# Attention scores from two float32r parts of queries and keys, in two row halves of the array

## The reference

```python
x = x + _L0_attn_ref(_layernorm(x, axis=-1), ...)     # retention
x = x + _L0_ffn_ref(_layernorm(x, axis=-1), ...)      # experts
x = x + _L1_attn_ref(_layernorm(x, axis=-1), ...)     # attention
x = x + _L1_ffn_ref(_layernorm(x, axis=-1), ...)      # routed tokens
# _L1_attn_ref: 16 heads of 8 numbers
q = (hidden_states @ Wq.T + bq).reshape(b, s, 16, 8) * 8 ** -0.5
k = (hidden_states @ Wk.T + bk).reshape(b, s, 16, 8)
v = (hidden_states @ Wv.T + bv).reshape(b, s, 16, 8)
scores = jnp.einsum('bqhd,bkhd->bhqk', q, k)
probs = jax.nn.softmax(scores, axis=-1)
out = jnp.einsum('bhqk,bkhd->bqhd', probs, v).reshape(b, s, d) @ Wo.T + bo
```

## Time and profile before

| | us |
|---|---|
| median of 3 runs (1101.86 to 1104.05) | 1103.3 |
| span of the profiled execution | 1072.1 |
| what lies around the span (the difference) | 31.2 |
| first fill of the stacks to last (L1164) | 469.9 to 927.2 |

### The profile page before, as it was taken

The page is one execution under the profiler, slowest core; times in us unless marked ns, Lnnn a source line. Parts: engine busy times, 40 slices in busy tenths (PEclk is TensorE's granted clock), DMA queues, the critical chain, the costliest instruction groups (busy, mean ns, idle before and its releaser), DMA issues. The chain is left out here.

```text
span 1072.1 us, 29674 instructions
## 1 busy us (share of the span) xinstructions
PE 963.4 (90%) x9857; PEld 717.1 (67%) x9858; DVE 706.6 (66%) x1509; ACT 640.7 (60%) x1320; POOL 707.7 (66%) x1531
## 2 busy tenths in 40 slices
PE   6999999689989999459999999999999999963776
PEld 5888888479956666335767777777777777632554
DVE  5778787685534444236788887788787788735752
ACT  4666766422224434126788888888888888762552
POOL 4677676467735555567688888888888888534003
PEclk9999999799999999757999999999999999996999
DMA  8600000131123332134444544445454445302000
GB/s 315 262 3 2 2 2 2 45 104 53 50 74 83 81 83 70 52 106 132 122 137 140 149 130 141 127 137 150 124 149 124 124 134 140 99 17 61 12 3 21
DMA packets 88837, 100.91 MB, mean 94 GB/s; under 512 B 10654, under 2 KB 74366, under 8 KB 88318
## 3 DMA queue, kind: packets, MB, share of 16 engines
q1 hardware_dynamic: 83454, 87.97, 27.9%
q0 software_dynamic: 5248, 11.15, 3.2%
HBM read 61.78 MB, written 36.47 MB: 92 GB/s over the span
## 5 line engine op out<-in xcount | busy, mean ns | idle before, releaser
L1344 DVE TENSOR_REDUCE a_neg_max<-a_slot 128x4 f32<-128x1024 f32 x256 | 306.5, 1218 | 107.8 <-PE a_slot L1487 83.3
L1432 ACT ACTIVATE a_pT<-a_slot 128x1024 f32<-128x1024 f32 x256 | 255.3, 1024 | 13.5 <-PE a_slot L1503 6.5
L1487 PE MATMUL a_slot<-a_k_stack,a_q_stack 72*128 72x256 bf16 x1024 | 157.9, 278 | 7.3 <-DMA a_k_stack<-part_dram 6.3
L1503 PE MATMUL a_slot<-a_q_stack,a_k_stack 75*128 75x256 bf16 x1024 | 151.0, 275 | 2.0 <-ACT a_pT L1432 0.7
L1518 PE MATMUL a_ps_o<-a_pT,a_v_pad 128*32 128x256 f32 x2048 | 141.6, 386 | 0.0
L1487 PEld LDWEIGHTS a_slot<-a_k_stack,a_q_stack 72*128 72x128 bf16 x1024 | 95.5, 99 | 51.9 <-issue 25.5
L704 POOL DMA_INDIRECT y_rows<-m_total,m_token x80 | 76.6, 957 | 66.3 <-ACT m_total L857 52.4
L1503 PEld LDWEIGHTS a_slot<-a_q_stack,a_k_stack 75*128 75x128 bf16 x1024 | 93.0, 98 | 35.5 <-ACT a_pT L1432 14.2
L326 DVE TENSOR_TENSOR r_score<-ps_score,r_decay 128x512 f32<-128x512 f32 x128 | 81.4, 678 | 7.7 <-PE ps_score L478 7.6
L1518 PEld LDWEIGHTS a_ps_o<-a_pT,a_v_pad 128*32 128x32 f32 x2048 | 64.7, 109 | 27.5 <-issue 13.0
L697 POOL DMA_INDIRECT sorted_in<-h,m_slot x64 | 63.9, 998 | 26.1 <-issue 18.9
(11 more groups left out here) (293 smaller groups left out, 2121.7 us busy)
## 6 DMA issues: line engine op xcount, KB each, us to landing
a_q_stack<-part_dram SPq DMA_DIRECT2D x64, 288.0 KB
a_k_stack<-part_dram SPq DMA_DIRECT2D x64, 288.0 KB
part_dram<-a_part SPq DMA_DIRECT2D x64, 192.0 KB, 2.7
sorted_in<-h SPq DMA_DIRECT2D x10, 528.0 KB, 13.6
m_xe<-sorted_in SPq DMA_DIRECT2D x40, 132.0 KB, 2.2
expert_up<-in_eu_dram SPq DMA_DIRECT2D x1, 4096.0 KB, 25.1
part_dram<-a_part SPq DMA_DIRECT2D x64, 64.0 KB, 3.6
out_dram<-e_x_plus_h SPq DMA_DIRECT2D x32, 128.0 KB, 2.5
```

Of the source, the lines that this page charges most:

```text
L1344: nc.vector.tensor_reduce(neg_max[:, p, half, t, g * UNIT:(g + 1) * UNIT], slots[SLOT_OF["m", j]][:], AX.X, ALU.max, negate=True).then_inc ...
L1432: nc.scalar.activation(pT[:, j % PT_RING], slots[SLOT_OF["e", j]][:], ACT.Exp).then_inc(e_read, 1)
L1487: ins = nc.tensor.matmul(slots[SLOT_OF["m", j]][:, q], q_stack[0:QK_ROWS, p, half, head, t * P:(t + 1) * P], k_stack[0:QK_ROWS, p, half, h ...
L1503: ins = nc.tensor.matmul(slots[SLOT_OF["e", j]][:, q], k_stack[0:EXP_ROWS, p, half, head, t * P:(t + 1) * P], q_stack[0:EXP_ROWS, p, half, ...
```

## The change

- [...] The four products of parts take 4 x 8 = 32 rows; one row of zeros against ones follows (`MAX_ROWS` = 33), and two rows of maximum parts against ones (`EXP_ROWS` = 35).
- The 8 heads of a half are dealt to two row halves of the array (`TILES` = 2): rows 0 to 34 and rows 64 to 98 of the stacks. `scores` (L1490 of the new file) issues, for each group, the four matmuls alternately for the upper and the lower half; the two of a pair write different banks of the slot. The number of matmuls and their 128 x 256 output stay.
- The stacks and the DRAM buffers hold float32, 4 bytes for 2. A half's fill is four DMAs of 128 KB (two for `q_stack`, two for `k_stack`) instead of two of 288 KB. Keys and queries have a DRAM tensor each (`k_dram`, `q_dram`); a half's store is two DMAs of 64 KB for keys and one of 128 KB for queries, instead of one of 64 KB and one of 192 KB. A half's maxima take two DMAs instead of one.
- `k_stack` is filled from `k_dram` with the broadcast as the outermost dimension: the source is 2 (step 0) x 16 x 1024, the destination 32 rows x 1024. The source of `q_stack` is 16 x 2 (step 0) x 1024. Before, the sources were 24 x 3 x 2048 for both.
- `fill_ones` moves ahead of the first fill; the heads' order in the weights (`by_half`) follows the new layout; `ident_b` goes, since the maxima are transposed in float32.

```diff
 HH = AH // HALVES
-PARTS = 3
+PARTS = 2
 PAIRS = PARTS * PARTS
 QK_ROWS = PAIRS * AD
-EXP_ROWS = QK_ROWS + PARTS
+MAX_ROWS = QK_ROWS + 1
+EXP_ROWS = MAX_ROWS + PARTS
+TILES = 2
+TILE_ROWS = P // TILES
+HT = HH // TILES
 UNIT = 4
+UT = UNIT // TILES
 M_UNITS = AH // UNIT * TPS
 PT_RING = 4
...
         qk = m.sbuf("a_qk", [P, 2, 2, S])
-        rest = m.sbuf("a_rest", [P, 2, S])
-        part = m.sbuf("a_part", [P, 2, 2, PARTS, S], BF16)
-        SLOTS = 2 * PARTS + PARTS - 1
-        part_dram = nc.dram_tensor("part_dram", (2, HALVES, SLOTS, AD, HH, S), BF16, kind="Internal").ap()
-        q_stack = m.sbuf("a_q_stack", [P, 2, HALVES, HH, S], BF16)
-        k_stack = m.sbuf("a_k_stack", [P, 2, HALVES, HH, S], BF16)
+        part = m.sbuf("a_part", [P, 2, 2, PARTS, S])
+        q_dram = nc.dram_tensor("q_dram", (2, HALVES, PARTS, AD, HH, S), F32, kind="Internal").ap()
+        k_dram = nc.dram_tensor("k_dram", (2, HALVES, AD, PARTS, HH, S), F32, kind="Internal").ap()
+        q_stack = m.sbuf("a_q_stack", [P, 2, HALVES, HT, S])
+        k_stack = m.sbuf("a_k_stack", [P, 2, HALVES, HT, S])
...
-        max_rest = m.sbuf("a_max_rest", [P, TPS, HH])
-        max_part = m.sbuf("a_max_part", [P, HALVES, TPS, PARTS, HH], BF16)
-        max_T = m.sbuf("a_max_T", [PARTS * HH, HALVES, S], BF16)
+        neg_max = m.sbuf("a_neg_max", [P, 2, HALVES, TPS, TILES, HH // UNIT, UT])
+        max_part = m.sbuf("a_max_part", [P, HALVES, TPS, TILES, PARTS, HT])
+        max_T = m.sbuf("a_max_T", [PARTS * HH, HALVES, S])
         pT = m.sbuf("a_pT", [P, PT_RING, UNIT, S])
...
 
-        FILLS = 2
+        FILLS = 2 * TILES
+        STORES = 1 + PARTS
...
-                        for half in range(HALVES):
-                            sp.dma_start(k_stack[QK_ROWS:EXP_ROWS, q, half],
-                                         ones_b[:].unsqueeze(1).to_broadcast([PARTS, HH, S])).then_inc(ones_in, 16)
+                    sp.wait_ge(preset, 5)
+                    for tile in range(TILES):
+                        at = tile * TILE_ROWS
+                        sp.dma_start(k_stack[at + QK_ROWS:at + EXP_ROWS].rearrange("r p h g s -> r (p h g) s"),
+                                     zero_ones[:].unsqueeze(1).to_broadcast([1 + PARTS, 2 * HALVES * HT, S])
+                                     ).then_inc(ones_in, 16)
+                        sp.dma_start(q_stack[at + QK_ROWS:at + MAX_ROWS].rearrange("r p h g s -> r (p h g) s"),
+                                     zero_ones[0:1].unsqueeze(1).to_broadcast([1, 2 * HALVES * HT, S])).then_inc(ones_in, 16)
 
             def store_parts(s, p, r):
-                slots = lambda half, first, end: part_dram[p, half, first:end].rearrange("a d h s -> (d h) a s")
-                rows = lambda half: part[half * HH * AD:(half + 1) * HH * AD, p].rearrange("r w a s -> r (w a) s")
-                after(sp, part_step, 8 * s + 4)
+                rows = lambda half, which: part[half * HH * AD:(half + 1) * HH * AD, p, which]
+                after(sp, part_step, 2 * PARTS * s + PARTS)
                 for half in range(HALVES):
                     after(sp, filled[p][half], twice(8 * FILLS, r))
-                    sp.dma_start(slots(half, 2 * PARTS, SLOTS), rows(half)[:, PARTS:2 * PARTS - 1]
+                    for a in range(PARTS):
+                        sp.dma_start(k_dram[p, half, :, a], rows(half, 1)[:, a]
+                                     ).then_inc(part_stored[p][half], 16)
+                after(sp, part_step, 2 * PARTS * (s + 1))
+                for half in range(HALVES):
+                    sp.dma_start(q_dram[p, half].rearrange("a d h s -> (d h) a s"), rows(half, 0)
                                  ).then_inc(part_stored[p][half], 16)
-                after(sp, part_step, 8 * (s + 1))
-                for half in range(HALVES):
-                    sp.dma_start(slots(half, 0, 2 * PARTS), rows(half)).then_inc(part_stored[p][half], 16)
 
             def fill(half):
 
                 def step(s, p, r):
                     after(sp, e_filled, ((s - 2) * 4 + 2 * half + 2) * (M_UNITS // 8) * 2)
-                    after(sp, part_stored[p][half], twice(16, r + 1))
-                    sp.dma_start(q_stack[0:QK_ROWS, p, half],
-                                 part_dram[p, half, 0:PARTS].rearrange("a d h s -> (a d) (h s)").unsqueeze(1)
-                                 .to_broadcast([PARTS * AD, PARTS, HH * S])).then_inc(filled[p][half], 16)
-                    sp.dma_start(k_stack[0:QK_ROWS, p, half],
-                                 bass.AP(part_dram.tensor, part_dram[p, half, PARTS].offset,
-                                         [[HH * S, PARTS * AD], [AD * HH * S, PARTS], [1, HH * S]])
-                                 ).then_inc(filled[p][half], 16)
+                    after(sp, part_stored[p][half], 16 * STORES * (r + 1))
+                    for tile in range(TILES):
+                        rows, heads = slice(tile * TILE_ROWS, tile * TILE_ROWS + QK_ROWS), slice(tile * HT, (tile + 1) * HT)
+                        sp.dma_start(q_stack[rows, p, half],
+                                     q_dram[p, half, :, :, heads].rearrange("a d h s -> (a d) (h s)").unsqueeze(1)
+                                     .to_broadcast([PARTS * AD, PARTS, HT * S])).then_inc(filled[p][half], 16)
+                        sp.dma_start(k_stack[rows, p, half],
+                                     k_dram[p, half, :, :, heads].rearrange("d a h s -> (d a) (h s)").unsqueeze(0)
+                                     .to_broadcast([PARTS, PARTS * AD, HT * S])).then_inc(filled[p][half], 16)
                 return step
 
             def give_max(half):
                 def step(s, p, r):
                     after(sp, maxT_copied, HALVES * s + half + 1)
-                    sp.dma_start(q_stack[QK_ROWS:EXP_ROWS, p, half], max_T[:, half]).then_inc(max_in[p][half], 16)
+                    for tile in range(TILES):
+                        at = tile * TILE_ROWS
+                        sp.dma_start(q_stack[at + MAX_ROWS:at + EXP_ROWS, p, half],
```

```diff
@@ -1241,13 +1254,12 @@
                 inv_std_of(s, p, stats3_done, mv3, ve3, minus_mean3, ve3_done, rstd3, rstd3_done, shift3, shift3_done,
                            h3_done)
 
-            def split(steps, at, value, left, high, mid, low, shape):
+            def split(steps, at, value, high, low, shape):
 
                 none = zeros[:].unsqueeze(1).to_broadcast(shape) if len(shape) == 3 else zeros[:].to_broadcast(shape)
-                for n, (to, a, b, op) in enumerate(((high, value, none, ALU.add), (left, value, high, ALU.subtract),
-                                                    (mid, left, none, ALU.add), (low, left, mid, ALU.subtract))):
-                    nc.gpsimd.tensor_tensor(to, a, b, op).then_inc(steps, 1)
-                    after(pool, steps, at + n + 1)
+                nc.gpsimd.tensor_tensor(high.bitcast(F32R), value, none, ALU.add).then_inc(steps, 1)
+                after(pool, steps, at + 1)
+                nc.gpsimd.tensor_tensor(low.bitcast(F32R), value, high, ALU.subtract).then_inc(steps, 1)
...
+            def scores(slot, rows, weights, moving, of_weights, p, half, g):
+                for r in range(UT):
+                    for tile in range(TILES):
+                        at = slice(tile * TILE_ROWS, tile * TILE_ROWS + rows)
+                        ins = nc.tensor.matmul(slot[:, tile * UT + r], weights[at, p, half, g * UT + r, of_weights].bitcast(F32R),
+                                               moving[at, p, half, g * UT + r].bitcast(F32R), start=True, stop=True)
+                return ins
+
...
                     if j % 4 == 0:
                         after(pe, filled[p][half], 16 * FILLS * (r + 1))
                     free_slot("m", j, s)
-                    for q in range(UNIT):
-                        head = g * UNIT + q
-                        ins = nc.tensor.matmul(slots[SLOT_OF["m", j]][:, q],
-                                               q_stack[0:QK_ROWS, p, half, head, t * P:(t + 1) * P],
-                                               k_stack[0:QK_ROWS, p, half, head], start=True, stop=True)
-                    ins.then_inc(m_filled, 1)
+                    scores(slots[SLOT_OF["m", j]], MAX_ROWS, q_stack, k_stack, slice(t * P, (t + 1) * P), p, half, g
+                           ).then_inc(m_filled, 1)
                 return step
...
 
-    return np.ascontiguousarray(weight.reshape(-1, HALVES, HH, AD).transpose(0, 1, 3, 2).reshape(-1, D))
+    heads = weight.reshape(-1, HALVES, HH // UNIT, TILES, UT, AD)
+    return np.ascontiguousarray(heads.transpose(0, 1, 5, 3, 2, 4).reshape(-1, D))
```

58 lines of the change are left out of this document (26 added, 32 removed).

## The result

The changed kernel takes 1252.1 us (median of 4 runs, 1234.3 to 1267.3) where the kernel before, run beside it, takes 1102.6 (1101.8 to 1104.1). The ratio is **1.123**, 95% interval 1.118 to 1.128. Slower was forecast, and 1195 us with a range of 1130 to 1290: sign and range held, but the loss is 135 us by the ratio where 92 was forecast.

A forecast was written before the change was run, and what follows sets the result against it. PE was taken to bound the kernel before at 14.63 us a sample; the two-engine DMA loop would make it 17.6. Over 31 periods that adds 92 us to 1103.3: 1195 us, range 1130 to 1290.

The forecast's parts named there:

- the key fill on two engines: Attention phase: broadcast outermost, 2 against 32, puts each 128 KB key fill on two DMA engines, 2.75 us each.
- The group of scores at 0.22 us: PE's score groups: two float32r matmuls run side by side, so four take 0.22 us instead of 0.435.
- PE's own need, 12.8 us: PE's work per sample falls from about 14.1: -3.4 from paired score matmuls, about +2 from array shape changes.
- 14.1, with 11.9 as the lower end: SP's issue time for a turn's 19 DMAs, in us; 11.9 if each issue costs 0.62.
- In part of the time, it hides in the slack: Rival of PE becoming the bound, from 1290 us, chance 0.12: half clock only part of the time costs nothing.
- a granted clock well under 1: Sign in the attention phase that would point to the rival of PE becoming the bound, chance 0.12.
- 3 us or more a sample: Sign that the forecast is right: PE's largest wait is for `a_k_stack` from `k_dram`, of this size.
- the size of the loop: Fills, stores and waits on the two DMA engines sum to 17.8 us a sample; 17.6 used.
- the idle terms (2.3 for issue and start, 1.0 for landing): Parts of the two-engine DMA loop, in us a sample, when no data flows on the engines.
- The forecast's own bound for engines that are never idle, 14.5 to 15.5: Two-engine DMA loop per sample, in us, if no issue or landing time left the engines idle.
- The first rival: Key fills spread like query fills, so SP or PE decides: 1087 or 1062 us; chance 0.13, 0.10 of it faster.
- Its third branch: With key fills spread wide, SP's waits add to its 14.1 us of issues, giving 1110 us; slower, 0.02.

The follow-up runs named there:

- e4: Kernel before with the key fill's two outer source dimensions swapped, 3 outermost and 24 inside; ratio 1.035, median 1147.6 us.
- e1: Changed kernel with keys stored in three DRAM slots, so key fills walk 16 rows outermost instead of 2; ratio 1.003, median 1107.1 us.
- e7: Kernel of e1 with all four matmuls of a score group on the first half's rows (0 to 34); ratio 1.212, median 1317.9 us.
- e8: Kernel of e1 with SP issuing the second half's maxima before the query stores and the output; ratio 0.998 to the kernel before.
- e9: Changed kernel with, from the second sample on, two of four matmuls in each score group and half of `values`; ratio 1.117, median 1232.1 us.
- e10: Kernel of e8 with, from the second sample on, two of four matmuls in each score group and half of `values`; ratio 1.063, median 1173.2 us.
- e11: Kernel of e8 with three PE steps moved later: the maxima's transposes, `project_qk` and `transpose_h`; ratio 1.016 to the kernel before.
- e12: Kernel of e8 with only `project_qk` and the first half's maxima transposes moved later; ratio 0.9965 to the kernel before.
- e2: Kernel of e1 with the loops over `tile` and `r` swapped, changing the order of a group's four matmuls; ratio 1.007, median 1117.7 us.

## Why the prediction was right, and where it was not

**Right, as forecast.**
- The step that decided, the key fill on two engines: read at 0.13 in the profile, repeated with three engines at 0.19 in e4, and without it (e1) the loss is gone. The phase's mean rate fell as forecast too, to about 100 GB/s.
- The group of scores at 0.22 us: 0.24 with another group behind it in the same shape (704.57 to 704.81 in e1), 0.34 where the weights of its first matmuls are exposed (701.64 to 701.98). By e7 it is the pair that saves. The 2x of the Trainium skill, TensorEngine Tiling (Array Packing), section Theoretical Speedup, is nearly reached within a group: 0.44 to 0.24.
- PE's own need, 12.8 us: in e8 each step at its shortest sums to 12.8 (values 4.0, eight groups at 0.34 and eight at 0.24 make 4.6, projections, output and transposes 4.2). Against the 14.1 of before the groups save 7.0 - 4.6 = 2.4 (16 at 0.44 before) and the other steps cost 1.1 more: -1.3, where -3.4 and +2 were forecast.
- POOL: L1260 and L1262 take 12.9 + 16.1 + 4.7 + 4.9 = 38.6 us in some 11 samples, 3.5 each against 6.9 before.
- SP: an issue of a fill costs about 0.60 us, a store 0.64, a maximum 0.69, some 12.0 us in all; the forecast took 14.1, with 11.9 as the lower end. SP waits 5.8 us a sample (62.9 in 200 us) and isn't the bound. For the kernel before the forecast's own terms sum to about 8 us and the trace has 8.1, not "about 9"; nothing else was built on that.

**Wrong, the clock.** "In part of the time, it hides in the slack" is the step that failed. It treated the fill wait and the half clock as things that lie side by side. They follow each other: PE waits for a fill (the 0.91 us at 799.35), then it is granted half the clock, and at half clock it is itself the bound, with nothing to hide under (busy 16.97 of 17.10 us). 6.95 us at half clock times 0.42 or 0.43 is 2.9 to 3.0 us a sample, some 83 us in 28 samples. It was given 0.12 as a rival and belonged in the main case. Of the forecast's own signs, "a granted clock well under 1" came out, and "3 us or more a sample" of waiting for `a_k_stack` did not: PE waits 1.3 to 1.5 us.

**Wrong, the size of the loop.** The sum said 17.6 us. With the clock's part taken off, the line through the samples leaves 15.9. The fills add 1.3 us of idle PE a sample to e1's 0.6, and e9 against e10 says 1.6 us. One engine's rate was priced about right (20.4 to 23.9 GB/s forecast, 21 to 26 read); that leaves the idle terms (2.3 for issue and start, 1.0 for landing) as too long. Perhaps q fills, stores and `y_rows` keep the two engines fed between key fills; that is argued, and no run shows it. The forecast's own bound for engines that are never idle, 14.5 to 15.5, was the nearer one. The 15.9 is a fit, not an experiment: no run has the two-engine fills with a clock that stays full. e9 and e10 are the nearest to it, at one low clock.

**Wrong, what is left when the fills are quick.** The first rival gave 1062 to 1087 us for fills over sixteen engines, from PE's 13.3 or SP's 14.1; on the chip it is 1.003 of the kernel before. Its third branch, 1110 us "if SP's waits add to its 14.1", meets e1's 1107 by number and not by cause, since SP isn't the bound. PE's need did fall by 1.3 us, but e1's and e8's samples take 14.7 and 14.6: the saving turned into 1.8 us of gaps between PE's steps, most of them before uses of `a_ps_misc`. The forecast counted PE's waits with 0.5 us. e11 and e12 show that the gaps move with the order of the steps.

**Two errors met.** For the loop +3.0 us was forecast and the fit gives about +1.3; for the clock nothing was forecast and the fit gives +3.0. 17.6 and 18.9 us (mean of the first 28) look near only because the errors cancel in part. That the time fell in the range is in part luck: the cause of the loss was right, its way into the time was not.

Open: where all of the 11.2 us before the first `by_token` come from. The first fill is issued at 488.5 us in the changed kernel and at 488.7 in e1, and the first scores follow 9.1 and 4.9 us later, so 4 us are that fill; the other 7 lie behind it and are not taken apart. Open too: why e2's order makes no difference; and what exactly holds 14.3 us in e12, where PE's need is 12.8.

## What to carry to other kernels

Where a DMA's broadcast stands outermost, count that dimension: 2 there put 128 KB on two engines of sixteen and cost 12%, and a third stored copy that lets 16 stand outermost gave all of it back with as many DMAs. A new wait on PE is not to be priced by its length alone: look at what the clock was granted after such waits elsewhere in the trace, and add the price that traces show (here 0.40 to 0.44 us for each us at half clock) wherever PE would be the bound. A line through period against time at half clock takes the waits in with the clock, so give the idle time a term of its own. And a smaller PE need is worth only what the bank that its steps share lets through, so find the steps that end later than their shortest before counting a saving.

## What was not expected of the hardware

- PE can be busy 100% of a stretch, never waiting, and be granted 0.50 (e7: 62.2 us with matmuls on one half of the rows), while the same instructions ran at 1.00 in another stretch of e7, and e1's, on two halves, at 1.00 throughout the first 28 samples.
- Taking half of the score matmuls and half of `values` away made the kernel 6.5% slower (e8 to e10), through a granted clock of 0.57.
- Four matmuls ordered half 0, half 0, half 1, half 1 start in pairs just as if they alternated (e2: 0, 7, 224, 229 ns).
- Two chips ran the same kernel at 1076 and 1104 us; e1 and e8 put 20 us of that ahead of the first `by_token`.
